# A graph network on one core: the column chunks of four layers become six of 504 and one of 101, without loops

## What is computed

```
agg_x = segment_sum(x[src], dst, num_segments=n) + x
agg_e = segment_sum(edge_attr @ ew.T + eb, dst, num_segments=n) + eb
h = concatenate([agg_x, agg_e], axis=1) @ w1.T + b1
h = relu((h - mean(h)) * rsqrt(var(h) + BN_EPS) * bn_w + bn_b)
return h @ w2.T + b2
```

## Time and profile before

| | |
|---|---|
| median of 3 runs | 686.85 us (686.78 to 686.87) |
| the profiled execution | 684.61 us |
| its span, first to last instruction | 682.8 us |
| mean granted TensorE clock | 0.959 |
| TensorE, VectorE, ScalarE busy | 618.4, 345.8, 262.5 us |
| TensorE on the chain that ended last | 57% of the span |

### The profile page before, as it was taken

The page is one execution under the profiler, slowest core; times in us unless marked ns, Lnnn a source line. Parts: engine busy times, 40 slices in busy tenths (PEclk is TensorE's granted clock), DMA queues, the critical chain, the costliest instruction groups (busy, mean ns, idle before and its releaser), DMA issues.

```text
span 682.8 us, 13708 instructions
## 1 busy us (share of the span) xinstructions
PE 618.4 (91%) x5319; PEld 383.1 (56%) x5319; DVE 345.8 (51%) x837; ACT 262.5 (38%) x569; POOL 61.8 (9%) x90
## 2 busy tenths in 40 slices
PE   4788898988999979799997999997999998999976
PEld 3676677754555534755554755556655548555546
DVE  6788999989999937612112521204412125210124
ACT  1266966755666624701013510106201027010133
POOL 5640032410110100000000000000000000000000
PEclk9788999999999999999998999999999998999998
DMA  6961000000000000010000100000100000100033
GB/s 183 324 205 8 3 28 3 5 5 4 4 3 5 4 4 3 1 32 1 1 0 1 31 0 0 0 0 0 30 0 0 0 0 0 32 1 2 0 94 95
DMA packets 13305, 18.97 MB, mean 28 GB/s; under 512 B 2263, under 2 KB 7397, under 8 KB 13251
## 3 DMA queue, kind: packets, MB, share of 16 engines
q1 hardware_dynamic: 12099, 16.00, 7.7%
q0 software_dynamic: 1152, 2.20, 1.4%
HBM read 16.26 MB, written 1.60 MB: 26 GB/s over the span
## 4 chain that ended last, share of the span: by engine, by line
PE 57%; DVE 3%; ACT 1%; issue 1%; POOLq 0%; DVEq 0%
PE bank L1275 38%; PE bank L1338 10%; PE bank L1310 7%; PE bank L1304 2%; DVE bn_stats L1497 1%; ACT h L1391 1%; DVE h L1518 0%; ACT aggT L1382 0%; DVE h L1519 0%; PE bank L230 0%; ACT bn_small L1404 0%; PE bank L1321 0%; DVE h L1538 0%; DVE bound_row L1477 0%; DVE bn_small L1512 0%
## 5 line engine op out<-in xcount | busy, mean ns | idle before, releaser
L1275 PE MATMUL bank<-adj,h_pieces 128*128 (+1 forms) x1372 | 265.4, 353 | 0.0
L1275 PEld LDWEIGHTS bank<-adj,h_pieces 128*128 128x128 f16 x1372 | 133.1, 97 | 131.6 <-issue 8.7
L1497 DVE BATCH_NORM_STATS2 bn_stats<-bank 128x6 f32<-128x450 f32 (+1 forms) x70 | 43.8, 629 | 228.7 <-PE bank L1310 224.8
L935 ACT ACTIVATE adj<-bank 128x450 bf16<-128x450 f32 x175 | 96.0, 549 | 78.0 <-PE bank L800 63.2
L1382 ACT ACTIVATE aggT<-bank 128x450 f32<-128x450 f32 x28 | 15.3, 546 | 270.6 <-PE bank L1310 237.9
L421 DVE TENSOR_TENSOR h<-iota_lo,h 128x768 bf16<-128x768 bf16 (+1 forms) x182 | 101.6, 558 | 5.8 <-PE bank L800 4.4
L824 PE MATMUL bank<-h,adj 128*17 128x40 f32 (+11 forms) x1752 | 84.2, 207 | 15.7 <-DVE h L613 9.6
L824 PEld LDWEIGHTS bank<-h,adj 128*17 128x17 f32 x1752 | 73.0, 104 | 23.2 <-DVE h L613 13.2
L800 PEld LDWEIGHTS bank<-h 128*128 128x128 bf16 x1064 | 51.7, 100 | 60.6 <-DVE h L421 46.3
L800 PE MATMUL bank<-h 128*128 128x75 bf16 x1064 | 70.3, 203 | 16.6 <-DVE h L421 14.6
L430 PE MATMUL bank<-adj,h_pieces 128*128 128x450 bf16 x343 | 83.6, 356 | 1.6 <-issue 1.6
(11 more groups left out here) (147 smaller groups left out, 323.1 us busy)
## 6 DMA issues: line engine op xcount, KB each, us to landing
adj<-attr SPq DMA_DIRECT2D x1, 2524.5 KB
adj<-attr SPq DMA_DIRECT2D x1, 1963.5 KB
weights<-wpack SPq DMA_DIRECT2D x5, 323.0 KB
out<-h SPq DMA_DIRECT2D x6, 256.0 KB
adj<-attr SPq DMA_DIRECT2D x1, 1402.5 KB, 6.8
adj<-attr SPq DMA_DIRECT2D x2, 561.0 KB
h<-mpack SPq DMA_DIRECT2D x5, 179.0 KB
adj<-order SPq DMA_DIRECT2D x2, 202.0 KB
```

What stands on the lines that cost most here:

```text
L935: nc.scalar.activation(out_view(u), bank_view(n % CNT_BANKS), ACT.Copy).then_inc(s_ev, 1)
L1275: last = nc.tensor.matmul(agg_ps[b][:, 0:CW], hp[:, k, s, :], adj[:, k, ds(c * CW, CW)], start=(k == 0 and s == 0), stop=stop and s == pie ...
L1497: V.bn_stats(stats[:, h, ds(c * 6, 6)], w1_ps[b][h][:, 0:cols]).then_inc(st_last if last and h == 1 else st_done, 1)
```

## The change

It gives the chunks another width. `LW` = 504, `WIDTHS` = six times 504 and one 101, 3125 in all: padding columns aren't computed. The first part keeps chunks of 450. The loops over layers 1 to 3 and over chunks become Python loops, so all code is written out and column addresses are constants. The sums of the last chunk go to a buffer of their own, the first row of `bound_row`, which is free after `w2_scaled`; their evacuation waits for that and no longer for the hidden products of chunk 5. The order of the steps on each engine stays.

```
+LW = 504
+WIDTHS = [min(LW, N_NODES - c * LW) for c in range(CHUNKS)]
...
-            aggT = sb(ctx, "aggT", [P, max(CW, 2 * D)], F32)
+            aggT = sb(ctx, "aggT", [P, LW], F32)
...
+            def sums_of(c):
+                return aggT[:, 0:WIDTHS[c]] if c < CHUNKS - 1 else row[:, 0, 0:WIDTHS[c]]
...
-                                last = nc.tensor.matmul(agg_ps[b][:, 0:CW], hp[:, k, s, :], adj[:, k, ds(c * CW, CW)],
+                                last = nc.tensor.matmul(agg_ps[b][:, 0:w], hp[:, k, s, :], adj[:, k, c * LW:c * LW + w],
                                                         start=(k == 0 and s == 0), stop=stop and s == pieces_of(k)[-1])
...
-                            nc.tensor.matmul(w1_ps[b][h][:, 0:CW], m6[:, h * P:(h + 1) * P], s6[:, ds(c * CW, CW)],
+                            nc.tensor.matmul(w1_ps[b][h][:, 0:w], m6[:, h * P:(h + 1) * P], s6[:, c * LW:c * LW + w],
                                              start=True, stop=False)
...
-                        sums_in = aggT[:, 0:CW] if later(l) else agg0[:, c * CW:(c + 1) * CW]
+                        sums_in = sums_of(c) if later(l) else agg0[:, c * LW:c * LW + w]
...
-                        with pe.Fori(1, CHUNKS // 2) as i:
-                            aggregate(l, 2 * i + 1, 1)
-                            hidden(l, 2 * i, 0)
-                            aggregate(l, 2 * i + 2, 0)
-                            hidden(l, 2 * i + 1, 1)
+                        for c in range(3, CHUNKS):
+                            aggregate(l, c, c % 2)
+                            hidden(l, c - 1, (c - 1) % 2)
                         hidden(l, CHUNKS - 1, 0)
...
-                    with pe.Fori(1, LAYERS - 1) as l:
+                    for l in range(1, LAYERS - 1):
                         layer(l, False)
...
-                    def evac_agg(l, c, b):
+                    def evac_agg(l, c, b, final):
                         n = (l - 1) * CHUNKS + c
                         act.wait_ge(agg_done, n + 1)
-                        if not (isinstance(c, int) and c == 0):
+                        if 1 <= c < CHUNKS - 1:
 
                             act.wait_ge(w1_done, (l * CHUNKS + c) * 2)
-                        nc.scalar.activation(aggT[:, 0:CW], agg_ps[b][:, 0:CW], ACT.Copy).then_inc(agg_ev, 1)
+                        if c == CHUNKS - 1 and not final:
+                            act.wait_ge(w2_scaled, l + 1)
+                        nc.scalar.activation(sums_of(c), agg_ps[b][:, 0:WIDTHS[c]], ACT.Copy).then_inc(agg_ev, 1)
...
-                            last = nc.scalar.activation(h1[:, h, ds(c * CW, CW)], w1_ps[b][h][:, 0:CW], ACT.Identity,
+                            last = nc.scalar.activation(h1[:, h, c * LW:c * LW + WIDTHS[c]], w1_ps[b][h][:, 0:WIDTHS[c]], ACT.Identity,
                                                         bias=wp[:, B1 + h:B1 + h + 1])
...
-                            v = h1[:, h, u * UW:min((u + 1) * UW, COLS)]
+                            v = h1[:, h, u * UW:min((u + 1) * UW, N_NODES)]
...
-                        cols = N_NODES - (CHUNKS - 1) * CW if last else CW
+                        cols = WIDTHS[c]
```

More of the change, by code:

```diff
@@ L215, in units, with rest_view @@
             return view[:, 4 * u:min(4 * u + 4, NODE_TILES)]
-        def rest_view(c):
-            return h1[:, 0, :].bitcast(BF16)[:, ds(c * (2 * CW), CW)]
+        def rest_view(c, w):
+            return h1[:, 0, :].bitcast(BF16)[:, ds(c * (2 * LW), w)]
         l_c = sem("consts_loaded")
@@ L1053, in _ @@
                                 sp.wait_ge(s_gfree, c * NODE_TILES + k + 1)
[L1054 removed]
+                                sp.dma_start(rest_view(0, CW), rest_dram[:, ds(k * COLS + c * CW, CW)]).then_inc(s_gload, 16)
                     @block.gpsimd
@@ L1137, in _ @@
                                 for s in pieces_of(k):
-                                    last = nc.tensor.matmul(agg0_ps[0][:, 0:CW], hp[:, k, s, :], rest_view(0), start=False,
+                                    last = nc.tensor.matmul(agg0_ps[0][:, 0:CW], hp[:, k, s, :], rest_view(0, CW), start=False,
                                                             stop=(k == NODE_TILES - 1))
@@ L1240, in load_layer @@
                         with sp.If(general > 0):
-                            with sp.Fori(0, CHUNKS) as c:
+                            for c, w in enumerate(WIDTHS):
                                 with sp.Fori(0, NODE_TILES) as k:
                                     sp.wait_ge(rest_free, ((l - 1) * CHUNKS + c) * NODE_TILES + k + 1)
-                                    sp.dma_start(rest_view(c), rest_dram[:, ds(k * COLS + c * CW, CW)]
+                                    sp.dma_start(rest_view(c, w), rest_dram[:, ds(k * COLS + c * LW, w)]
                                                  ).then_inc(rest_loaded, 16)
@@ L1266, in aggregate @@
                     def aggregate(l, c, b):
-                        n = (l - 1) * CHUNKS + c
-                        if not (isinstance(c, int) and c < 2):
+                        n, w = (l - 1) * CHUNKS + c, WIDTHS[c]
+                        if c >= 2:
                             pe.wait_ge(agg_ev, n - 1)
@@ L1278, in aggregate @@
                         for k in range(NODE_TILES - 1):
-                            if isinstance(c, int) and c == 0 and k % 4 == 0:
+                            if c == 0 and k % 4 == 0:
                                 pe.wait_ge(hp_done, l * UNITS + k // 4 + 1)
                             products(k, False)
-                        if isinstance(c, int) and c == 0:
+                        if c == 0:
                             pe.wait_ge(hp_done, (l + 1) * UNITS)
@@ L1288, in aggregate @@
                                 for s in pieces_of(k):
-                                    last = nc.tensor.matmul(agg_ps[b][:, 0:CW], hp[:, k, s, :], rest_view(c),
+                                    last = nc.tensor.matmul(agg_ps[b][:, 0:w], hp[:, k, s, :], rest_view(c, w),
                                                             start=False, stop=False)
@@ L1296, in hidden @@
                     def hidden(l, c, b):
-                        if isinstance(c, int) and c == 0:
+                        w = WIDTHS[c]
+                        if c == 0:
                             pe.wait_ge(m_done, l + 1)
                             pe.wait_ge(w1_scaled, l + 1)
-                        if not (isinstance(c, int) and c < 2):
+                        if c >= 2:
                             pe.wait_ge(h1_ev, l * CHUNKS + c - 1)
                         for h in range(2):
-                            nc.tensor.matmul(w1_ps[b][h][:, 0:CW], m6[:, h * P:(h + 1) * P], s6[:, ds(c * CW, CW)],
+                            nc.tensor.matmul(w1_ps[b][h][:, 0:w], m6[:, h * P:(h + 1) * P], s6[:, c * LW:c * LW + w],
                                              start=True, stop=False)
@@ L1307, in hidden @@
                             pe.wait_ge(agg_ev, (l - 1) * CHUNKS + c + 1)
-                        sums_in = aggT[:, 0:CW] if later(l) else agg0[:, c * CW:(c + 1) * CW]
+                        sums_in = sums_of(c) if later(l) else agg0[:, c * LW:c * LW + w]
                         for h in range(2):
-                            nc.tensor.matmul(w1_ps[b][h][:, 0:CW], wp[:, W1A + h * P:W1A + (h + 1) * P], sums_in,
+                            nc.tensor.matmul(w1_ps[b][h][:, 0:w], wp[:, W1A + h * P:W1A + (h + 1) * P], sums_in,
                                              start=False, stop=True).then_inc(w1_done, 1)
@@ L1414, in layer @@
                         act.wait_ge(l_wp, (l + 1) * 16)
[L1415 to L1420, removed]
+                        evac_agg(l, 0, 0, final)
+                        for c in range(1, CHUNKS):
+                            evac_agg(l, c, c % 2, final)
+                            evac_h1(l, c - 1, (c - 1) % 2)
                         evac_h1(l, CHUNKS - 1, 0)
@@ L1426, in _ @@
                     normalise(0, False)
-                    with act.Fori(1, LAYERS - 1) as l:
+                    for l in range(1, LAYERS - 1):
                         layer(l, False)
@@ L1557, in _ @@
                     layer(0, False)
-                    with dve.Fori(1, LAYERS - 1) as l:
+                    for l in range(1, LAYERS - 1):
                         layer(l, False)
```

2 lines of the change are left out of this document (1 added, 1 removed).

## The result

| | before | after |
|---|---|---|
| median of 7 runs (lowest to highest) | 686.87 us (685.92 to 690.27) | 681.89 us (680.27 to 684.24) |
| the profiled execution | 684.61 | 680.31 |
| its span | 682.8 | 678.5 |
| the five projections, sum | 65.22 | 66.31 |
| from layer 0's first product to the end, less these | 360.76 | 355.99 |

The ratio is 0.9913, 95% interval 0.9886 to 0.994: 5 us faster, where I had forecast 2. The time lies 0.7 us under my range. With seven runs of the kernel before in place of the three that I had seen, its own scatter is 4.4 us and not 0.1.

The account below looks back on a forecast made before the run. TensorE was taken to bound the kernel, mostly by the aggregation's products. Fixed sum -3.0 and clock +1.1 gave -1.9 us, from 686.85 to 684.9 us; range 682.6 to 688.4.

Parts of the forecast that it names:

- The products: Aggregation on TensorE: six chunks of 10.41 us and one of 2.25 for seven of 9.31, -0.45 us a layer.
- The rule that I had weighed: Short aggregation chunk: at 81 ns a product it would take 4.0 us, +1.7 a layer, sum +5.0; not adopted.
- The hidden products: Six chunks' hidden products before the end of the last but one grow from 1.89 to 2.11 us, +1.34 a layer.
- The tail: From the last but one hidden chunk's end (T) to the square root: 2.16 us for 3.73, -1.57 a layer.
- The fixed sum: All terms but the clock: -0.68 us a layer over four layers, -0.3 in layer 0, together -3.0 us.
- The clock: TensorE's wait before projections grows from 3.7 to 4.0 us, risking further clock falls: +1.1 us, ends -2.5 and +4.5.
- The first rival: Before the projections: most boundaries' clocks fall and return late, +2.5 to +4.5 us, total 686.3 to 688.3; chance 0.26.
- Loops, branch, buffer: Removed loops and register work cost 0, as does the new buffer's wait; the branch before product 49 was a rival.
- the second rival: Branch between products 48 and 49 of the short chunk becomes visible: up to 1.5 us a layer, 690.9; chance 0.12.

Follow-up runs that it names:

- last_two: The changed kernel with widths of five times 504, 404 and 201: median 681.0 us, ratio 0.9895 to the kernel before.
- more_evac: The changed kernel with both short evacuations of the last chunk done twice, the second time into unused columns: 686.09 us, ratio 0.9971 to the kernel before.
- unroll_only: The kernel before with only its code written out, still 450 columns and shared aggT: 689.33 us, ratio 1.0018 to the kernel before.
- the second set: A later set of runs, with the changed kernel measured again unaltered beside the kernel before: 683.59 us, ratio 0.9932.
- fill_after_split: The changed kernel with 16 unread products before each projection, residual load in two parts and VectorE's wait for it moved: 673.54 us, ratio 0.9776 to before.
- fill_after: The changed kernel with 16 unread products in TensorE's wait before each projection: 674.75 us, ratio 0.9799 to the kernel before.
- fill_before: The kernel before, with 16 unread products in TensorE's wait before each projection: 677.43 us, ratio 0.9844 to it without them.

## Why the prediction was wrong

- **The products.** 10.42 and 2.21 us for 10.41 and 2.25: right. The 49 short products come every 45 ns. The rule that I had weighed ("TensorE: Matmul & The Clock Gate" of the Trainium skill, section Back-to-back issue gap), with some 81 ns at 128 columns for such a stream, doesn't hold here: the trace has 45 ns at 101 columns and, in last_two, 4.25 us / 49 = 87 ns at 201. In proportion between them that is some 56 ns at 128, an estimate.
- **The hidden products.** 2.12 us a chunk: right. By the chains of layer 1, a layer's first product to T is 77.56 before (288.17 to 365.73) and 78.43 after (289.84 to 368.27), +0.87 where I had -0.45 + 1.34 = +0.89.
- **The tail: here the forecast failed.** The step was "0.68 + 0.71 + 2 x 0.36 + 0.05 = 2.16 for 3.73", a saving of 1.57. The order of the work in it was right, the size wrong: 1.78 us for 2.16, a saving of 1.95. I had priced the three evacuations at 0.71 + 0.72 = 1.43 us, and they take 1.03 us from the first's start to the square root. The long one is 0.68, but in a row each hides some 0.1 us of itself behind the next, which the pair of 1.16 us for two of 636 ns had shown, and I used that for the short ones only, with the price of another operation. more_evac has measured it: 0.235 for 0.36.
- **The fixed sum.** -1.08 us a layer for -0.68, in four layers -4.3 for -2.7; layer 0 -0.42 for -0.3 (19.82 us from its first product to its projection before, 19.40 after). Together -4.8 where I had -3.0. With the tail at its size the sum would have been -4.8 + 1.1, about 683.2, inside the range. The last 1.3 us to 681.89 are start of layer 0 and scatter of the medians, for which the range left little room.
- **The clock.** +1.1 was forecast, +1.09 was found in the profile (66.31 for 65.22), and layer 0, which had been spared, was not spared. That is luck: layer 0 rose by 2.71 us (11.53 to 14.24), more than the 2.5 that I had as the most, and the next three fell by 1.6 together. The second profile of the same kernel had 65.22. What is shown is that the falls before the projections cost some 8 to 9 us in either kernel (8.1 before, 9.0 and 7.9 in the change, against 57.3 and 57.1 with the filling). The first rival, with the clock taking the gain, is wrong.
- **Loops, branch, buffer.** unroll_only has the loops at nothing (+0.3 us in the profile, ratio 1.0018 with 0.9996 to 1.0039). The branch before product 49 does not show in a chunk of 2.21 us, so the second rival is wrong. The own buffer pays.
- **The median.** Between the medians lie 5.0 us, between the two profiles 4.3: -4.8 for the rest, +1.1 for the projections, and -0.6 for the earlier start of layer 0, which is scatter of the first part. Each median carries some such scatter; in the second set the change was 4.5 us under before.

## What to carry to other kernels

Cutting work unevenly so that the last piece is short doesn't remove work but moves it ahead of the join. What it gains is decided by the follow-up work of the last long piece, not of the short one. Price that work instruction by instruction, each at its pace in a row and not at its own record's length. The shortest last piece need not be the best: 404 and 201 columns gave 0.2 us a layer more than 504 and 101. When a tail gets shorter, see which engine ends it then (here ScalarE, with a longer last piece VectorE, and at last a load that had been hidden). And where TensorE waits for some microseconds before dense work, look at the clock of that work first: unread products in the wait were worth nearly twice the change.

## What I had not expected of the hardware

- The same first part, with the same instructions, ended anywhere between 256.2 and 261.2 us. That is as wide as the scatter of the runs of one kernel. What lies behind it, less the projections, was 355.98 to 356.05 in three profiles with the change's chunks and 360.76 and 360.82 in the two of the kernel before with and without filling; fill_after_split, with its late store, had 356.74.
- After waits of 3.4 to 4.1 us the projection took 12.9 to 14.3 us in nearly every layer of every kernel without filling; layer 0 of the kernel before and of unroll_own kept 11.53, the time at full clock. And 16 products of 504 columns in the wait ended this each time, in ten of ten waits of fill_after and fill_before.
